# Decoder kernel, first self attention: projections as three products of rounded halves, weights split in the first batch and kept in memory

## The chip, the core and the metric

One core of a Trainium2 chip runs the whole program. The metric is the device time of one execution in microseconds; three runs of the kernel before gave 2879.1, 2882.16 and 2884.32, median 2882.16 us.

## What is computed

The model is a decoder of two layers over x of (4, 512, 512). The change touches only the first stage, the self attention of layer 0:

```python
q = x @ Wq + bq
k = x @ Wk + bk
v = x @ Wv + bv
q, k, v = (to_heads(q), to_heads(k), to_heads(v))
scores = jnp.einsum('bdsh,bdth->bdst', q, k) / SCALE
weights = jax.nn.softmax(scores, axis=-1)
feats = jnp.einsum('bdst,bdth->bdsh', weights, v)
feats = feats.transpose(0, 2, 1, 3).reshape(B, S, F)
return feats @ Wo + bo
```

Behind it come a cross attention, a mixture of experts, a second self and cross attention and a ternary feed-forward, all as before.

## The kernel before

`self_attention_0` runs the stage for one batch of 512 rows after the other (B = 4); the last batch is written out apart from the loop. All engines run their own program and meet in semaphores; the order of the work is that in which each engine's code is written.

**Projections.** For each batch there are twelve groups of products (g = 0 to 11): four of queries, four of keys (PARTS = 8 together), four of values. TensorE sums a group over four blocks of the contraction (L254, L257), in float32, into one of two banks, `mm[g % 2]`; it may start group g when the bank of g-2 has been read (`s.mm.free`). VectorE reads the bank with the bias added into `whole[:, g % 2]` (L401, L403). ScalarE rounds it to `high` (float32r, L340) and makes the copies that the scores need (L344): one half of `q_parts` per head, or both halves of `k_high`. VectorE subtracts `high` from `whole` (L391) into the low half of `q_parts`, or twice per head into `k_low`. This subtraction for group g-1 stands in VectorE's program in front of the reading of bank g. Value groups are added to `v_rows` directly (L407).

**Attention.** 32 tiles (`TILES`, 8 heads by 4) of scores, each as two products (L267, L268), maximum on VectorE (L411), exponential on ScalarE (L354), turned by TensorE (L109), weighted sums (L290), then the output projection (L316), which already uses three products of rounded halves (`feats_high`, `feats_low`, `wo_high`, `wo_low`) and is read on VectorE at L459. At the end of each but the last batch the next batch's x is turned and ScalarE copies it to `x_cols` (L332). VectorE ends a batch with the layernorm, for which GpSimd makes the root (L96).

**Transfers.** SP issues all loads of the stage at the start: x of batch 0, the three weights, all of x (4 MB, `x_tok`), `Wo`, biases. In each batch it then reloads `x_rows` (L226), loads two blocks of the second layer's output weights (L215) and stores their split halves (L220). GpSimd splits `Wo` in batch 0, then copies the experts' weights from memory to memory (L787 to L791) and at last issues the clearing of `moe_sorted` (L479), with batches 1 to 3's roots behind it.

Of the kernel before, what the change touches and what calls it, by code (L numbers as in the profile page):

```python
# [27 lines left out]
P = 128  # L28
# [105 lines left out]
def self_attention_0(nc, m, x, Wq, bq, Wk, bk, Wv, bv, Wo, bo, packed, a):  # L134
# [17 lines left out]
    PARTS = 2 * KD  # L152
    NEXT_X = TILES + 6
    Q0, SC = NT, TILES + 2 * NT
    TA, TV, MM = TILES // 2, TILES // 2, 3 * KD + 2 * GROUPS + NT
    with ExitStack() as ctx:
        sb, sem = allocator(nc, ctx, "a0")
        wq, wk, wv = (sb(n, [P, KD, D]) for n in ("wq", "wk", "wv"))
# [3 lines left out]
        x_rows, x_cols = sb("x_rows", [P, NT, D]), sb("x_cols", [P, KD, S])  # L162
# [6 lines left out]
        turned = [sb(f"turned_{i}", [P, NT, S]) for i in range(TURNED - 2)] + [x_rows, x_cols]  # L169
        turned = [x_rows] + [t for t in turned if t is not x_rows and t is not x_cols] + [x_cols]  # L170
        spare = turned[1:TURNED - 1]
        wo = spare[2]
        feats_high, feats_low = q_parts[:, 0:KD, :], q_parts[:, KD:2 * KD, :]
        feats = sb("feats", [P, NT, D])
        zeros = sb("zeros", [P, LATENT])
# [11 lines left out]
        s.whole_ready, s.high_ready, s.high_done, s.low_done = (sem(n) for n in ("whole_ready", "high_ready", "high_done", "low_done"))  # L187
        s.var_ready, s.rstd_ready = sem("var_ready"), sem("rstd_ready")
# [5 lines left out]
        block = ctx.enter_context(nc.Block())  # L194

        @block.sync
        def _(sp):
# [25 lines left out]
            with sp.Fori(0, B - 1) as b:  # L223
# [10 lines left out]
        def _(pe):  # L234
# [8 lines left out]
            def batch(b, last_one):  # L243
                F0 = NT + TILES if last_one else TILES + 2 * NT
                pe.wait_ge(s.sc.free, b * SC + s.sc.size + Q0)
                for g in range(3 * KD):
                    pe.wait_ge(s.mm.free, b * MM + g + 1)
                    c = g % KD
                    if c == 0:
                        pe.wait_ge((w_q, w_k, w_v)[g // KD], 32)  # L250
# [8 lines left out]
                    last.then_inc(s.mm.full, 1)  # L259
                pe.wait_ge(s.high_done, b * PARTS + PARTS)  # L260
# [67 lines left out]
        def _(act):  # L328
            def keep_x(use):
                for j in range(NT):  # L330
                    act.wait_ge(s.sc.full, use + j + 1)
                    act.copy(x_cols[:, :, j * P:(j + 1) * P], blocks_of(sc[j], KD)).then_inc(s.sc.free, 1)  # L332

            def batch(b, last_one):
# [42 lines left out]
            with act.Fori(0, B - 1) as b:  # L377
                batch(b, False)
# [3 lines left out]
        def _(dve):  # L382
            with dve.Fori(0, B) as b:
# [83 lines left out]

        @block.gpsimd
        def _(pool):
            pool.wait_ge(w_out, 32)  # L470
# [8 lines left out]
            pool.dma_start(packed.sorted.rearrange("(t p) d -> p t d", p=P), zeros[:].unsqueeze(1).to_broadcast([P, packed.sorted_tiles, LATENT])) \  # L479
# [284 lines left out]
class Packed:  # L764


    def __init__(self, nc, ctx):
# [5 lines left out]
        self.qkv1 = nc.dram_tensor("split_qkv", ((HEADS1 + 2 * KV_HEADS1), P, 2, KD, HD1), F32, kind="Internal").ap()  # L773
        self.wo1 = nc.dram_tensor("split_out", (HEADS1, P, 2, D), F32, kind="Internal").ap()
# [2193 lines left out]
```

## Time and profile before

| What | us |
|---|---|
| runs, median (lowest, highest) | 2882.16 (2879.1, 2884.32) |
| span of the profiled execution | 2871.8 |
| median above the span | 10.4 |
| TensorE busy | 2673.5 (93%) |
| VectorE busy | 1806.2 (63%) |
| ScalarE busy | 1420.3 (49%) |
| GpSimd busy | 294.5 (10%) |
| projections of batch 0, first product to first score | 12.05 to 54.79 |

The profile states the span of its execution, from the first instruction to the last; a whole execution's time has what lies around it as well, and the page gives no other time for it. "PE" is TensorE, "DVE" VectorE, "ACT" ScalarE, "POOL" GpSimd, "SP" the engine that issues most transfers; a "q" behind a name is that engine's sequencer. A span is printed for the products of a group together, with the count behind "x"; a float32 product of 512 columns stands there as two records. The granted clock is a share of 2.4 GHz.

### The profile page before, as it was taken

Reading aid. Unit: us, or ns where it says so; the run is one execution under the profiler, and the core shown is the slowest. Engines: PE = TensorE matmul, PEld = TensorE weight load, DVE = VectorE, ACT = ScalarE, POOL = GpSimd, SP = SyncE. Lnnn points to the kernel's source line nnn. Section 1 sums busy time; section 2 is a strip of 40 time slices with the busy share of each in tenths; the row PEclk is TensorE's granted clock in tenths of the full one; section 3 lists DMA queues with packets and bytes.
Section 4 is the critical chain, followed back from the end, with each engine's and each line's share of the span. In section 5 each row is a group of like instructions: output and inputs, shape, how many; then the busy total and the mean of one; then the engine's idle time right before and its main releaser. Section 6 shows DMA issues by size and latency. Waiting matters only on the chain. (4 is left out here: it accounts for less than half of the span.)

```text
span 2871.8 us, 40570 instructions
## 1 busy us (share of the span) xinstructions
PE 2673.5 (93%) x12750; PEld 1685.2 (59%) x12750; DVE 1806.2 (63%) x3475; ACT 1420.3 (49%) x2978; POOL 294.5 (10%) x399
## 2 busy tenths in 40 slices
PE   8999997979999987999999999997999999997898
PEld 4555554444588863677777777775545455443444
DVE  5666674654543326756755756754777777775676
ACT  4454463322133322554553653743577676664665
POOL 1230003001711114000000000001110101000000
PEclk9999998989999999999999999998899999999999
DMA  3395105541687754323223223211000000001000
GB/s 140 86 123 143 58 15 184 186 141 54 200 277 234 248 184 148 115 103 109 73 106 110 68 104 124 66 67 59 5 6 6 5 2 5 2 2 71 26 23 30
DMA packets 114169, 266.30 MB, mean 93 GB/s; under 512 B 14464, under 2 KB 37008, under 8 KB 113200
## 3 DMA queue, kind: packets, MB, share of 16 engines
q1 hardware_dynamic: 97152, 211.16, 22.2%
q0 software_dynamic: 16816, 52.64, 7.8%
q8 instruction: 104, 1.70, 0.2%
q14 instruction: 97, 0.79, 0.1%
HBM read 208.97 MB, written 58.48 MB: 93 GB/s over the span
## 5 line engine op out<-in xcount | busy, mean ns | idle before, releaser
L2506 DVE TENSOR_REDUCE x_neg_max<-bank 128x1 f32<-128x512 f32 x512 | 327.1, 684 | 99.7 <-PE bank L2351 99.2
L2458 ACT ACTIVATE x_weights<-bank 128x512 f32<-128x512 f32 x512 | 279.1, 599 | 127.8 <-PE bank L2362 122.9
L1885 ACT ACTIVATE a_probs<-bank,a_neg_max 128x128 f32<-128x128 f32 (+3 forms) x256 | 136.1, 532 | 206.0 <-DVE a_neg_max L1979 202.0
L1785 PE MATMUL bank<-a_x_high,a_weights 128*128 128x512 f32 x640 | 218.3, 404 | 8.2 <-DMA a_weights<-split_qkv 2.3
L109 PEld LDWEIGHTS bank<-all_ident,a_probs 128*128 128x128 f32 x1200 | 151.5, 140 | 85.0 <-issue 47.0
L109 PE MATMUL bank<-all_ident,a_probs 128*128 128x128 f32 x1200 | 193.3, 273 | 3.0 <-ACT a_probs_t L1877 2.2
L1877 ACT COPY a_probs_t<-bank 128x128 f32<-128x128 f32 (+3 forms) x256 | 107.6, 420 | 144.2 <-PE bank L109 143.8
L1820 PE MATMUL bank<-a_k_cols,a_q_cols 128*128 128x128 f32 (+3 forms) x512 | 176.7, 434 | 0.4 <-DVE a_q_cols L1928 0.2
L1849 PE MATMUL bank<-a_wo,a_att_high 128*128 128x512 f32 x512 | 162.1, 398 | 3.9 <-DVE a_q_cols L1928 2.9
L1510 DVE TENSOR_TENSOR moe_acc<-bank,moe_acc 128x512 f32 x79 | 54.6, 692 | 171.1 <-PE bank L1176 170.5
L1165 PE MATMUL bank<-moe_gh_cols,moe_item 128*128 128x256 f32 x632 | 151.8, 383 | 3.0 <-DMA moe_item<-moe_items 2.7
L1176 PE MATMUL bank<-moe_item,moe_wide 128*128 128x256 f32 x632 | 149.4, 379 | 0.0
L1832 PE MATMUL bank<-a_probs_t,a_v_rows 128*128 128x512 f32 (+3 forms) x512 | 148.6, 433 | 0.0
L1264 ACT ACTIVATE moe_wide<-bank,moe_item 128x256 f32<-128x256 f32 x158 | 66.3, 471 | 161.6 <-PE bank L1165 129.1
L1785 PEld LDWEIGHTS bank<-a_x_high,a_weights 128*128 128x128 f32 x640 | 121.3, 189 | 39.6 <-issue 6.2
L1891 ACT ACTIVATE a_probs<-a_probs,a_inv_sum 128x128 f32<-128x128 f32 (+3 forms) x256 | 142.0, 555 | 2.7 <-DVE a_inv_sum L1984 2.7
L2351 PE MATMUL bank<-x_k_cols,x_q_cols 64*128 64x512 f32 x512 | 136.6, 498 | 3.5 <-DVE x_neg_max L2506 3.4
L1979 DVE TENSOR_REDUCE a_neg_max<-bank 128x1 f32<-128x128 f32 (+3 forms) x256 | 125.7, 491 | 18.8
L2384 PE MATMUL bank<-x_weights,x_v_rows 128*17 128x512 f32 x1024 | 135.7, 603 | 0.0
L1165 PEld LDWEIGHTS bank<-moe_gh_cols,moe_item 128*128 128x128 f32 x632 | 118.1, 191 | 22.9 <-DMA moe_item<-moe_items 7.4
L2362 PE MATMUL bank<-x_q_cols,x_k_cols 64*128 64x512 f32 x512 | 128.1, 419 | 3.2 <-ACT x_weights L2458 2.8
L1176 PEld LDWEIGHTS bank<-moe_item,moe_wide 128*128 128x128 f32 x632 | 119.9, 190 | 16.8 <-issue 0.3
(413 smaller groups left out, 5437.0 us busy)
## 6 DMA issues: line engine op xcount, KB each, us to landing
a_weights<-split_qkv SPq DMA_DIRECT2D x80, 512.0 KB, 3.6
moe_item<-moe_items SPq DMA_DIRECT2D x79, 257.0 KB, 3.8
moe_item<-moe_items SPq DMA_DIRECT2D x79, 256.0 KB, 3.7
a_wo<-split_out SPq DMA_DIRECT2D x8, 2048.0 KB, 7.8
a_wo<-split_out SPq DMA_DIRECT2D x16, 1024.0 KB, 9.9
split_qkv<-x_qkv_parts SPq DMA_DIRECT2D x12, 1024.0 KB, 5.1
moe_items<-in_L_ffn_e_w POOLq DMA_DIRECT2D x40, 256.0 KB
split_out<-a_turned SPq DMA_DIRECT2D x8, 1024.0 KB, 4.0
```

What stands on the lines that cost most here:

```text
L109: last = pe.transpose(bank[:, c * P:(c + 1) * P], rows[:, c * P:(c + 1) * P], ident)
L1165: last = pe.matmul(bank(("hidden", i))[:, c * TOKENS:(c + 1) * TOKENS], weight[:, k, c * P:(c + 1) * P], x_now[:, i % 2, k * TOKENS:(k + 1 ...
L1176: last = pe.matmul(bank(("item", i))[:, j * LATENT:(j + 1) * LATENT], hid[:, i % 2, c * TOKENS + j * P:c * TOKENS + (j + 1) * P], weight[: ...
L1785: last = pe.matmul(mm[g % 2], weight[:, k, :], x[:, k, :], start=n == 0, stop=n == 3 * KD - 1)
L1820: pe.matmul(sc[n % 4][:, 0:t], q_cols[:, h % 2, j * P:t], k_cols[:, h // GROUP, 0:t], start=True, stop=True).then_inc(s.sc.full, 1)
L1832: last = pe.matmul(mm[g % 2][:, c * P:], v_rows[:, c, kv * HD1:(kv + 1) * HD1], probs_t[:, n % 2, c, c * P:], start=c == 0, stop=c == NT - 1)
L1849: last = pe.matmul(mm[g % 2], att[:, at, j * P:(j + 1) * P], wo[:, at, part, :], start=h == first and att is att_high and part == 0, stop= ...
L1885: act.activation(probs[:, n % SLOTS, 0:t], sc[n % 4][:, 0:t], ACT.Exp, bias=neg_max[:, n:n + 1], accum_out=row_sum[:, n:n + 1]).then_inc(s ...
L1891: act.activation(probs[:, i % SLOTS, 0:t1], probs[:, i % SLOTS, 0:t1], ACT.Copy, scale=inv_sum[:, i:i + 1]).then_inc(s.probs_ready, 1)
L2351: pe.matmul(score_banks[slot % 3], q_cols[rows, u % 2, pair, j * P:(j + 1) * P], k_cols[rows, u % 2, pair, :], start=True, stop=True).then ...
L2458: act.activation(weights[:, chunk % 2, k, :], weight_banks[slot % 2], ACT.Exp).then_inc(s.weight.free, 1)
L2506: dve.tensor_reduce(neg_max[:, g % 2, j, h:h + 1], score_banks[slot % 3], AX.X, ALU.max, negate=True) \
```

## The change

The three projections are computed as high·high + low·high + high·low: x is kept as `x_high` (ScalarE, float32r) and `x_low` (VectorE, the remainder), each weight as twelve pieces of two halves (pieces 0 to 3 of `Wq`, 4 to 7 of `Wk`, both by columns; 8 to 11 of `Wv`, by rows). A buffer of five slots, `pieces`, holds them: piece p lives in slot p % 5. In batch 0, which is now written out apart, ScalarE rounds each piece and VectorE subtracts; five pieces are made at the start and piece g+5 after group g. SP stores each made piece to `split_qkv0` in memory, and a slot is made anew only when its old piece is stored. For batches 1 to 3 SP loads the pieces from there: 0 to 4 after group 11 of the batch before, g+5 after group g. The raw `Wq` and `Wk` land in buffers used later for turned weights, `Wv` in `probs`. A value group needs all of pieces 8 to 11.

Besides: for keys ScalarE makes two of the four half copies, then signals `high_ready`, then makes the other two; the cast to `high` is gone there. VectorE writes `k_low` for only one half of the partitions, the other half is zeroed once. `x_low` is made on VectorE in step 41 of the 48 of the attention loop. The clearing of `moe_sorted` writes the same 6 MB in runs of 512 bytes instead of 1 KB.

```diff
-        wq, wk, wv = (sb(n, [P, KD, D]) for n in ("wq", "wk", "wv"))
+        pieces = sb("pieces", [P, PIECE_SLOTS, 2, D], F32R)
...
-        x_rows, x_cols = sb("x_rows", [P, NT, D]), sb("x_cols", [P, KD, S])
+        x_rows, x_high = sb("x_rows", [P, NT, D]), sb("x_high", [P, KD, S], F32R)
+        with ExitStack() as until_turned:
+            last_turned = until_turned.enter_context(nc.sbuf_tensor("a0_last_turned", [P, NT, S], F32))
+        x_low = sb("x_low", [P, KD, S], F32R)
...
+        wq, wk, wo = spare
+        wv = probs[:, 0:KD, :]
...
+            def load_piece(p):
+                sp.dma_start(pieces[:, p % PIECE_SLOTS].rearrange("p l n -> p (l n)").bitcast(F32), packed.qkv0[p].rearrange("p l n -> p (l n)")) \
+                  .then_inc(s.piece_in[p % PIECE_SLOTS], 16)
+
+            def next_pieces(b):
+                sp.wait_ge(s.mm.full, b * MM + PIECES)
+                for p in range(PIECE_SLOTS):
+                    load_piece(p)
+
+            def rest_of_pieces(b):
+                for p in range(PIECE_SLOTS, PIECES):
+                    sp.wait_ge(s.mm.full, b * MM + p - PIECE_SLOTS + 1)
+                    load_piece(p)
...
+            for p in range(PIECES):
+                sp.wait_ge(s.piece_in[p % PIECE_SLOTS], p // PIECE_SLOTS * 16 + 16)
+                sp.dma_start(packed.qkv0[p].rearrange("p l n -> p (l n)"), pieces[:, p % PIECE_SLOTS].rearrange("p l n -> p (l n)").bitcast(F32)) \
+                  .then_inc(s.piece_out[p % PIECE_SLOTS], 16)
+            for i in range(PIECE_SLOTS):
+                sp.wait_ge(s.piece_out[i], held(i) * 16)
+            next_pieces(0)
+            between(0)
+            with sp.Fori(1, B - 1) as b:
+                rest_of_pieces(b)
+                next_pieces(b)
+                between(b)
+            rest_of_pieces(B - 1)
...
+                def piece_ready(p):
+                    slot = p % PIECE_SLOTS
+                    pe.wait_ge(s.piece_in[slot], b * (held(slot) * 16) + p // PIECE_SLOTS * 16 + 16)
...
+                    if g < PARTS:
+                        piece_ready(g)
                     for k in range(KD):
-                        if g < PARTS:
-                            w = (wq, wk)[g // KD]
-                            last = pe.matmul(mm[g % 2], w[:, k, c * P:(c + 1) * P], x_cols[:, k, :],
-                                             start=k == 0, stop=k == KD - 1)
-                        else:
-                            last = pe.matmul(mm[g % 2], x_cols[:, k, c * P:(c + 1) * P], wv[:, k, :],
-                                             start=k == 0, stop=k == KD - 1)
+                        if g == PARTS:
+                            piece_ready(PARTS + k)
+                        for n, (w_part, x_part) in enumerate(((0, x_high), (0, x_low), (1, x_high))):
+                            start, stop = k == 0 and n == 0, k == KD - 1 and n == 2
+                            if g < PARTS:
+                                last = pe.matmul(mm[g % 2], piece_part(g, w_part)[:, k, :], x_part[:, k, :], start=start, stop=stop)
+                            else:
+                                last = pe.matmul(mm[g % 2], x_part[:, k, c * P:(c + 1) * P], piece_part(PARTS + k, w_part), start=start, stop=stop)
...
+            def high_piece(p):
+                if p in (0, KD, PARTS):
+                    act.wait_ge((w_q, w_k, w_v)[p // KD], 32)
+                if p >= PIECE_SLOTS:
+                    act.wait_ge(s.mm.full, p - PIECE_SLOTS + 1)
+                    act.wait_ge(s.piece_out[p % PIECE_SLOTS], p // PIECE_SLOTS * 16)
+                act.copy(piece_part(p, 0), raw_piece(p)).then_inc(s.piece_high, 1)
+
+            def batch(b, last_one, first_one=False):
                 F0 = NT + TILES if last_one else TILES + 2 * NT
                 for g in range(PARTS):
                     act.wait_ge(s.whole_ready, b * PARTS + g + 1)
-                    if g >= 2:
-                        act.wait_ge(s.low_done, b * PARTS + g - 1)
-                    act.copy(high[:, g % 2, :], whole[:, g % 2, :]).then_inc(s.high_ready, 1)
-                    for u in range(2):
-                        for half in range(2 if g >= KD else 1):
-                            to = k_high if g >= KD else q_parts
-                            last = act.copy(to[half * HD:(half + 1) * HD, 2 * (g % KD) + u, :], whole[u * HD:(u + 1) * HD, g % 2, :])
-                    last.then_inc(s.high_done, 1)
+                    if g < KD:
+                        if g >= 2:
+                            act.wait_ge(s.low_done, b * PARTS + g - 1)
+                        act.copy(high[:, g % 2, :], whole[:, g % 2, :]).then_inc(s.high_ready, 1)
+                        for u in range(2):
+                            last = act.copy(q_parts[0:HD, 2 * g + u, :], whole[u * HD:(u + 1) * HD, g % 2, :])
+                        last.then_inc(s.high_done, 1)
+                    else:
+                        for other in range(2):
+                            for u in range(2):
+                                half = (u + other) % 2
+                                last = act.copy(k_high[half * HD:(half + 1) * HD, 2 * (g % KD) + u, :], whole[u * HD:(u + 1) * HD, g % 2, :])
+                            last.then_inc((s.high_ready, s.high_done)[other], 1)
+                    if first_one and g + PIECE_SLOTS < PIECES:
+                        high_piece(g + PIECE_SLOTS)
...
+            def low_x(b):
+                for j in range(NT):
+                    tile = slice(j * P, (j + 1) * P)
+                    dve.wait_ge(s.x_high_ready, b * NT + j + 1)
+                    dve.tensor_tensor(x_low[:, :, tile], blocks_of(sc[j], KD), x_high[:, :, tile].bitcast(F32), ALU.subtract).then_inc(s.sc.free, 1)
+
+            def low_piece(p):
+                dve.wait_ge(s.piece_high, p + 1)
+                dve.tensor_tensor(piece_part(p, 1), raw_piece(p), piece_part(p, 0).bitcast(F32), ALU.subtract) \
+                   .then_inc(s.piece_in[p % PIECE_SLOTS], 16)
...
-                            for to in ([q_parts[HD:P, head, :]] if g <= KD else [k_low[0:HD, head, :], k_low[HD:P, head, :]]):
-                                last = dve.tensor_tensor(to, whole[rows, (g - 1) % 2, :], high[rows, (g - 1) % 2, :].bitcast(F32), ALU.subtract)
+                            to, part = (q_parts[HD:P, head, :], high[rows, (g - 1) % 2, :]) if g <= KD else (k_low[0:HD, head, :], k_high[rows, head, :])
+                            last = dve.tensor_tensor(to, whole[rows, (g - 1) % 2, :], part.bitcast(F32), ALU.subtract)
...
+                    if first_one and g + PIECE_SLOTS < PIECES:
+                        low_piece(g + PIECE_SLOTS)
                 for i in range(TILES + FEATS_LAG + 1):
+                    if i == NEXT_X + NT - 1 and not last_one:
+                        low_x(b + 1)
...
-            pool.dma_start(packed.sorted.rearrange("(t p) d -> p t d", p=P), zeros[:].unsqueeze(1).to_broadcast([P, packed.sorted_tiles, LATENT])) \
+            pool.dma_start(packed.sorted.rearrange("(p t) (u d) -> p (t u) d", p=P, u=2), zeros[:].unsqueeze(1).to_broadcast([P, 2 * packed.sorted_tiles, LATENT // 2])) \
```

ScalarE at the start of the stage and in the first query groups, before:

```order
L332 COPY a_x_cols<-bank 128x4x128 x4
L377 UNCONDITIONAL_BRANCH
L377 ISA
L340 CAST a_high<-a_whole 128x512
L344 CAST a_q_parts<-a_whole 64x512 x2
L337 REGISTER_ALU
L340 CAST a_high<-a_whole 128x512
L344 CAST a_q_parts<-a_whole 64x512 x2
L337 REGISTER_ALU
```

and now (`a_turned` there is the raw `Wq`, in one of the buffers of that name):

```order
L387 CAST a_x_high<-bank 128x4x128 x4
L395 CAST a_pieces<-a_turned 128x512 x5
L404 CAST a_high<-a_whole 128x512
L406 CAST a_q_parts<-a_whole 64x512 x2
L395 CAST a_pieces<-a_turned 128x512
L404 CAST a_high<-a_whole 128x512
L406 CAST a_q_parts<-a_whole 64x512 x2
L395 CAST a_pieces<-a_turned 128x512
L404 CAST a_high<-a_whole 128x512
```

The cast of a piece now stands behind each group's copies, in front of the cast to `high` of the next group.

SP from the last start loads on, before:

```order
L206 DMA all_x_tok<-in_x 128x16x512
L207 DMA a_turned<-in_L_attn_Wo 128x4x512
L208 DMA a_bo_row<-in_L_attn_bo 128x512
L223 UNCONDITIONAL_BRANCH
L225 ISA
L226 ISA
L226 DMA a_x_rows<-all_x_tok 128x2048
L212 ISA
L215 ISA
L215 DMA a_whole<-in_L_attn_Wo 128x2x512
L215 ISA
L215 DMA a_high<-in_L_attn_Wo 128x2x512
```

and now:

```order
L227 DMA all_x_tok<-in_x 128x16x512
L228 DMA a_turned<-in_L_attn_Wo 128x4x512
L229 DMA a_bo_row<-in_L_attn_bo 128x512
L267 DMA split_qkv<-a_pieces 128x1024 x12
L245 DMA a_pieces<-split_qkv 128x1024 x5
L261 DMA a_x_rows<-all_x_tok 128x2048
L236 DMA a_whole<-in_L_attn_Wo 128x2x512
L236 DMA a_high<-in_L_attn_Wo 128x2x512
L241 DMA split_out<-a_turned 128x2x1024 x2
L273 UNCONDITIONAL_BRANCH
```

Twelve stores of pieces stand behind the start loads, then the five loads for batch 1; in the loop seven more loads stand in front of these five.

## Rows read from the trace of the kernel before

**Rows 1.** the profile's page, part 1: busy us (share of the span) xinstructions

```profile
PE 2673.5 (93%) x12750; PEld 1685.2 (59%) x12750; DVE 1806.2 (63%) x3475; ACT 1420.3 (49%) x2978; POOL 294.5 (10%) x399
```

**Rows 2.** TensorE's timeline, batch 0: start us, us, engine, line, operation, count

```profile
12.05 13.97 PE L254 MATMUL bank<-a_x_cols,a_wq 128*128 128x512 f32 x32 [0.87 <-ACT a_x_cols L332]
...
54.79 0.79 PE L267 MATMUL bank<-a_k_high,a_q_parts 128*128 128x512 f32 x1
```

**Rows 3.** the same view, batch 1

```profile
123.79 13.89 PE L254 MATMUL bank<-a_x_cols,a_wq 128*128 128x512 f32 x32
137.52 13.90 PE L254 MATMUL bank<-a_x_cols,a_wk 128*128 128x512 f32 x32
...
166.95 0.79 PE L267 MATMUL bank<-a_k_high,a_q_parts 128*128 128x512 f32 x1
```

**Rows 4.** timeline, VectorE reading the output projection's banks, batch 0

```profile
115.59 0.69 DVE L459 TENSOR_TENSOR all_x_tok<-bank,all_x_tok 128x512 f32 x1 [0.16 <-PE bank L316]
...
118.40 0.68 DVE L459 TENSOR_TENSOR all_x_tok<-bank,all_x_tok 128x512 f32 x1
```

**Rows 5.** timeline, a key group (batch 0), then two query groups (batch 1)

```profile
34.00 0.75 DVE L403 TENSOR_SCALAR a_whole<-bank,a_bk_col 128x512 f32<-128x512 f32 x1 [0.24 <-issue]
...
35.36 2.50 ACT L344 CAST a_k_high<-a_whole 64x512 fp32r<-64x512 f32 x4
35.48 2.79 DVE L391 TENSOR_TENSOR a_k_low<-a_whole,a_high 64x512 fp32r<-64x512 f32 x4 [0.73 <-ACT a_high L340]
...
38.51 0.75 DVE L403 TENSOR_SCALAR a_whole<-bank,a_bk_col 128x512 f32<-128x512 f32 x1 [0.24 <-issue]
...
132.34 0.75 DVE L401 TENSOR_SCALAR a_whole<-bank,a_bq_col 128x512 f32<-128x512 f32 x1 [0.18 <-issue]
...
135.45 0.75 DVE L401 TENSOR_SCALAR a_whole<-bank,a_bq_col 128x512 f32<-128x512 f32 x1 [0.23 <-issue]
```

**Rows 6.** SP's issue, its landing, and 5 us windows (last: granted clock, DMA share, GB/s)

```profile
10.18 0.43 SPq L206 DMA_DIRECT2D all_x_tok<-in_x  x1
...
all_x_tok<-in_x SPq DMA_DIRECT2D x1, 4096.0 KB, 17.5
...
25.00:30.00 5.00, 5.00 (x13) 2.28 (x12) 3.12 (x5) 1.98 (x4) 0.00 (x0) 1.00 1.04 385
30.00:35.00 5.00, 5.00 (x13) 2.22 (x12) 3.74 (x6) 3.15 (x6) 0.00 (x0) 1.00 0.02 7
```

**Rows 7.** DMA issues from 300 to 310 us: KB each, us to landing

```profile
a_x_rows<-all_x_tok SPq DMA_DIRECT2D x1, 1024.0 KB, 5.2
```

**Rows 8.** timeline of GpSimd, and the landing of its last issue

```profile
127.03 0.95 POOL L787 DMA_DIRECT2D moe_items<-in_L_ffn_e_w  x1
...
238.67 2.28 POOL L479 DMA_DIRECT2D moe_sorted<-a_zeros  x1 [70.12 <-issue]
...
moe_sorted<-a_zeros POOLq DMA_DIRECT2D x1, 6144.0 KB, 22.7
```

**Rows 9.** SP's timeline; DMA issues and queues, 185 to 200, then 200 to 220 us

```profile
189.19 0.53 SPq L226 DMA_DIRECT2D a_x_rows<-all_x_tok  x1
...
q1 hardware_dynamic: 10, 0.08, 4.2%
a_x_rows<-all_x_tok SPq DMA_DIRECT2D x1, 1024.0 KB, 21.8
a_whole<-in_L_attn_Wo SPq DMA_DIRECT2D x1, 512.0 KB, 30.4
...
q1 hardware_dynamic: 580, 1.84, 58.1%
q0 software_dynamic: 619, 1.68, 51.9%
```

**Rows 10.** timeline of VectorE, end of batch 0's attention

```profile
107.89 0.69 DVE L427 COPY a_products<-bank 128x512 f32<-128x512 f32 x1 [4.11 <-PE bank L290]
```

**Rows 11.** window of 2 us, end of batch 1 (columns as in rows 6)

```profile
222.00:224.00 2.00, 1.64 (x8) 1.64 (x9) 1.43 (x3) 0.54 (x1) 0.00 (x0) 0.61 0.83 120
```

More of the change, by code:

```diff
@@ L152, in self_attention_0 @@
     PARTS = 2 * KD
+    PIECES, PIECE_SLOTS = 3 * KD, 5
     NEXT_X = TILES + 6
@@ L167, in self_attention_0 @@
         probs, products = sb("probs", [P, SLOTS, S]), sb("products", [P, S])
[L169 to L172, printed above, removed]
+        spare = [sb(f"turned_{i}", [P, NT, S]) for i in range(TURNED - 2)]
+        turned = [x_rows] + spare + [last_turned]
+        wq, wk, wo = spare
+        wv = probs[:, 0:KD, :]
         feats_high, feats_low = q_parts[:, 0:KD, :], q_parts[:, KD:2 * KD, :]
         feats = sb("feats", [P, NT, D])
-        zeros = sb("zeros", [P, LATENT])
+        zeros = sb("zeros", [P, LATENT // 2])
         out_rows = [whole[:], high[:].bitcast(F32)]
@@ L187, in self_attention_0 @@
         s.whole_ready, s.high_ready, s.high_done, s.low_done = (sem(n) for n in ("whole_ready", "high_ready", "high_done", "low_done"))
+        s.piece_in, s.piece_out = ([sem(f"{n}_{i}") for i in range(PIECE_SLOTS)] for n in ("piece_in", "piece_out"))
+        s.piece_high, s.x_high_ready, s.low_zeroed = sem("piece_high"), sem("x_high_ready"), sem("low_zeroed")
         s.var_ready, s.rstd_ready = sem("var_ready"), sem("rstd_ready")
@@ L194, in self_attention_0, with held, raw_piece, piece_part @@
         block = ctx.enter_context(nc.Block())
+        def held(slot):
+            return len(range(slot, PIECES, PIECE_SLOTS))
+        def raw_piece(p):
+            if p < PARTS:
+                return (wq, wk)[p // KD][:, :, p % KD * P:(p % KD + 1) * P]
+            return wv[:, p - PARTS, :]
+        def piece_part(p, part):
+            to = pieces[:, p % PIECE_SLOTS, part, :]
+            return to.rearrange("p (k n) -> p k n", k=KD) if p < PARTS else to
         @block.sync
@@ L221, in store_out, with between @@
                       .then_inc(s.out_stored, 16)
-            with sp.Fori(0, B - 1) as b:
+            def load_piece(p):
[9 more added lines that the diff above has]
+                    load_piece(p)
+            def between(b):
                 sp.wait_ge(x_tok_loaded, 16)
@@ L248, in batch @@
                     c = g % KD
[L249 to L250 removed]
+                    if g < PARTS:
+                        piece_ready(g)
                     for k in range(KD):
[L252 to L258 removed]
+                        if g == PARTS:
[6 more added lines that the diff above has]
+                                last = pe.matmul(mm[g % 2], x_part[:, k, c * P:(c + 1) * P], piece_part(PARTS + k, w_part), start=start, stop=stop)
                     last.then_inc(s.mm.full, 1)
+                pe.wait_ge(s.low_zeroed, 1)
                 pe.wait_ge(s.high_done, b * PARTS + PARTS)
@@ L331, in keep_x @@
                     act.wait_ge(s.sc.full, use + j + 1)
-                    act.copy(x_cols[:, :, j * P:(j + 1) * P], blocks_of(sc[j], KD)).then_inc(s.sc.free, 1)
-            def batch(b, last_one):
+                    act.copy(x_high[:, :, j * P:(j + 1) * P], blocks_of(sc[j], KD)).then_inc(s.x_high_ready, 1)
+            def high_piece(p):
[6 more added lines that the diff above has]
+            def batch(b, last_one, first_one=False):
                 F0 = NT + TILES if last_one else TILES + 2 * NT
@@ L376, in _ @@
             keep_x(0)
-            with act.Fori(0, B - 1) as b:
+            for p in range(PIECE_SLOTS):
+                high_piece(p)
+            batch(0, False, True)
+            with act.Fori(1, B - 1) as b:
                 batch(b, False)
@@ L382, in _, with batch @@
         def _(dve):
-            with dve.Fori(0, B) as b:
+            def low_x(b):
[7 more added lines that the diff above has]
+                   .then_inc(s.piece_in[p % PIECE_SLOTS], 16)
+            def batch(b, last_one, first_one=False):
                 for g in range(3 * KD):
@@ L466, in _ @@
                 layernorm(dve, st, b, m, s)
+            low_x(0)
+            for p in range(PIECE_SLOTS):
+                low_piece(p)
+            batch(0, False, True)
+            with dve.Fori(1, B - 1) as b:
+                batch(b, False)
+            batch(B - 1, True)
         @block.gpsimd
         def _(pool):
+            pool.memset(k_low[HD:P, :, :].bitcast(F32), 0.0).then_inc(s.low_zeroed, 1)
             pool.wait_ge(w_out, 32)
@@ L773, in __init__ @@
         self.qkv1 = nc.dram_tensor("split_qkv", ((HEADS1 + 2 * KV_HEADS1), P, 2, KD, HD1), F32, kind="Internal").ap()
+        self.qkv0 = nc.dram_tensor("split_qkv0", (3 * KD, P, 2, D), F32, kind="Internal").ap()
         self.wo1 = nc.dram_tensor("split_out", (HEADS1, P, 2, D), F32, kind="Internal").ap()
```

## The prediction

> **What bounds the kernel now.** The page's busy shares come first: TensorE is busy 93% of the span [rows 1], so the first question is whether the products of this change get shorter. The timeline of TensorE shows the projections of batch 0 from 12.05 us to the first scores at 54.79 [rows 2], those of batch 1 from 123.79 to 166.95; there four groups of query products (16 products, recorded as 32) take until 137.52, 3.43 us a group [rows 3]. What a group of three rounded products costs stands in the output projection, which is already written so: its banks are read at 115.59 and 118.40, 2.80 us for twelve products [rows 4]. So TensorE alone would gain 3.43 - 2.80 = 0.63 us a group, 7.6 a batch, 30 us in all.
>
> The next view says who really paces the groups. VectorE and ScalarE hand one buffer back and forth: VectorE makes `whole` (0.75), ScalarE rounds it (VectorE idles 0.73 for that; its half copies take 2.50 for four, 0.62 each), VectorE subtracts (2.79 for the four of a key group, 0.69 each; a query group has two) and only then takes the next bank. From `whole` to `whole` this is 3.11 us for queries and 4.51 for keys [rows 5]. In batch 1 VectorE starts late besides, behind the layernorm. So after batch 0 it is this chain that sets the pace, not TensorE, until the last value groups. I stepped groups, banks and this chain through with these durations: it gives 54.9 and 167.1 us for the two first scores, against 54.79 and 166.95 read. I use the same stepping below.
>
> **Batches 1 to 3, if every piece is there in time.** Query groups: the chain stays at 3.11, gain 0. Key groups: two low subtractions instead of four (-1.39), but `high_ready` now comes after two half copies instead of one cast (+0.62), so 4.51 - 0.77 = 3.74; four of them give 3.1. The last two value groups run on TensorE alone: 2 x 0.63 = 1.3. Together -4.2 us a batch (stepping: 162.7 instead of 166.95).
>
> **Batch 0.** Three things are added in front of or inside the chain.
> 1. Start. ScalarE casts piece 0 after its four copies, VectorE makes four `x_low` and low piece 0: first product at 13.2 instead of 12.05.
> 2. One more piece per group. For g = 0 to 6 ScalarE's cast of piece g+5 (0.62) and VectorE's subtraction (0.69) stand between `whole` and the next low part, and the cast stands behind all ScalarE copies of the group. A query step is 0.75 + 0.08 + 3 x 0.62 + 0.62 + 0.03 + 0.69 + 1.39 + 0.24 = 5.66, a key step 6.29. Stepping with this alone: first scores at 67.9, +13.0.
> 3. The wait for the store. Piece 5 goes into slot 0, so ScalarE must wait until piece 0 has been stored. SP puts this store behind all start loads in the same queue: the 4 MB load of x is issued at 10.18 and lands 17.5 us later, and the DMA engines run at 385 GB/s until 30 us and are idle behind that [rows 6]. 0.5 MB more at that rate is 1.4 us: I take 32 us for the first store. ScalarE is ready for it at about 19. While it stands there, the rounding of group 1 is queued behind it, VectorE waits in low piece 5, and TensorE stops when both banks are full, at 21.7. `whole` 1 ends at 35.8, `whole` 4 at 52.8, `whole` 7 at 71.7, the value groups end at 81.0.
>
> So the first scores of batch 0 move from 54.9 to 81.0: **+26.1**. Later stores have 5 us each and hold nothing up.
>
> **Batch 1: the pieces against GpSimd's copies.** SP loads pieces 5 to 11 (0.5 MB each) while the groups run, each after the group that frees its slot. In an empty queue that is harmless: 1 MB lands in 5.2 us [rows 7], and there are five groups (15 us) to spare for most, some 7 us for piece 11. But GpSimd starts its copies of the expert weights at 127.03, just as batch 1 begins, and their traffic holds its queue until 238.67 [rows 8]. What an SP load costs beside them: x_rows, issued at 189.19, lands after 21.8 us, the next 0.5 MB after 30.4; from 185 to 200 the SP queue moved 10 packets, from 200 to 220 1.84 MB, which is 92 GB/s [rows 9]. I take 9.5 us until a load begins, then 5.7 us a piece. Pieces 5 and 6 are issued before the copies have filled the queue. Piece 7, issued at 132.7, lands at 147.9, 8 at 153.6, 11 at 170.7. Value group 0 needs all of 8 to 11, so it ends at 171.4, and the scores start at 179.8 instead of 166.95: **+12.9**. The bounds: -4.2 if nothing is delayed, +27 at 8.5 us a piece (what the 0.5 MB behind took).
>
> Without the 9.5 us in front, still at 5.7 us a piece, piece 11 lands at 161.8, the scores start at 171.0 and the term is +4.0; that is for the rivals. The rows speak against it: 10 packets in 15 us, then 580 in 20 us beside 619 of the other queue [rows 9], so a load does wait before it gets its share.
>
> The Trainium skill, DMA: Bandwidth & Descriptors (Queues, rings and completion order), says that each engine takes turns between the queues at every packet. By that rule a piece would begin at once, which is the +4.0. The rows agree with turns after 200 us and not before.
>
> **The tail of batch 1.** Behind these come the five pieces of the next batch (28 us), x_rows and the two halves of the output weights on the same slow queue. x_rows then lands around 229, wanted at 228; the output weights around 241 to 248, wanted at 242. +4, bounds 0 and +10.
>
> **Batch 2.** The clearing of `moe_sorted` (6 MB, 22.7 us) is issued just at its start, at 238.67 [rows 8], and its source runs are halved to 0.5 KB. It is a memory write with nothing to wait for but the engines; a wait of 4.5 us in front of a piece costs under 1 us, one of 9.5 us gives +20. I take -3. **Batch 3** has no neighbour: -4.3.
>
> **Small terms.** `low_x` puts four subtractions into VectorE's gap of 4.11 us in front of the copy of `products` at 107.89 [rows 10]; the last of them must wait for ScalarE's last x copy and can push this copy by at most its own 0.69. I take half of it, three times: +1. GpSimd's clearing of half of `k_low` and its doubled run count are hidden before the first scores and behind batch 1. Clock: between 222 and 224 us, behind TensorE's gaps at the end of batch 1, the granted clock was 0.61 of full, so part of it at 1.2 GHz [rows 11]. Batch 0 leaves TensorE half idle; there the chain covers even groups at half clock (2 x 2.80 = 5.6 against 5.66), only the last value groups show it: +2, bounds 0 and 6.
>
> **Sum**: 26.1 + 12.9 + 4 - 3 - 4.3 + 1 + 2 = +38.7 us. The profile gives a span of 2871.8 us, 10.4 below the median of the runs; start and end are not touched, so the profiled execution stands for the median and I add to that: 2882.2 + 38.7 = **2920.9**.
>
> **Rivals.**
> - *TensorE paces after all* (faster). If the hand-over between VectorE and ScalarE did not bind, because `whole` and `high` have two buffers each, every group would give 0.63: 2882 - 30 = 2852. It decides once the chain is under 2.80 us a step. Against it: steps of 3.11 and 4.51 while both banks were full [rows 5]. Something faster than before by a few us also needs the store wait to vanish. 0.04.
> - *All transfers hidden.* The store of piece 0 overtakes, the pieces come in time: 13.0 - 12.7 + 1 = +1.3, 2883.5. For it: 0.5 MB alone is short. Against: the queue was never idle before 30 us, and the 4 MB load in front of the stores took its full 17.5 us [rows 6]. 0.07.
> - *Only the first store waits.* Batch 1's pieces get their share at once (+4.0) or are not delayed (-4.2), no tail: 26.1 + 4.0 - 3 - 4.3 + 3 = +26 down to +17: 2899 to 2908. 0.17.
> - *The contention is worse.* 8.5 us a piece in batch 1, +10 in the tail, or +20 in batch 2: 2940 to 2965. GpSimd's next layernorm step stands behind the clearing, which is issued only when the copies have drained; if more SP traffic stretches these, batch 2 starts late too. 0.17.
> - *Forecast* as above, 2908 to 2940: 0.55.
>
> **How the numbers follow.** About 0.2%, 6 us, is what a measurement of this kernel can tell from no change. Faster comes from the first rival alone, 0.04. No change: the second, 0.06, its rest being slower by a little. Slower: 0.90. The range must hold 8 in 10: it leaves out the first two rivals and the end of the fourth, and goes from 2892 to 2950.
>
> **What would show it.** In the new profile: the first scores of batch 0 near 81 us, with ScalarE idle from 19 to 32 in front of the cast of `pieces`, released by a DMA; group steps of 5.7 and 6.3 us behind that. Groups of 2.80 us on TensorE with gaps between them. In batch 1 a wait of 15 to 20 us in front of the first value group, released by a DMA into `pieces`; landings of 15 us and more there and under 5 in batch 3. Batch 3's projections 4.3 us shorter than before. The forecast is wrong if the first stores land before 25 us, if the pieces of batch 1 land in under 8 us, or if the stages behind the first attention change their length.

## The result, and the profile after

| | median us | lowest to highest | runs |
|---|---|---|---|
| before | 2883.24 | 2879.1 to 2892.22 | 4 |
| changed | 2917.08 | 2915.11 to 2921.52 | 4 |

The ratio is 1.0122, 95% interval 1.0101 to 1.0143: slower by 1.2%. The forecast was 2920.9 us in a range of 2892 to 2950, slower with 0.90. It held, but against the profiled execution of the kernel before two of its terms were too small and something else made up for them, as the stages show.

The span of the changed kernel's profiled execution is 2913.6 us. Its page, part 1, answers [rows 1]:

```profile
PE 2659.1 (91%) x12942; PEld 1728.9 (59%) x12942; DVE 1802.9 (62%) x3471; ACT 1419.1 (49%) x2974; POOL 299.6 (10%) x400
```

Windows by stage: first self attention, all up to the second cross attention, this, the rest. The kernel before (us, busy time and count of each engine, granted clock, DMA share, GB/s):

```profile
0.00:469.70 469.70, 434.55 (x1809) 246.64 (x1809) 310.87 (x492) 226.61 (x492) 58.90 (x81) 0.99 0.41 92
469.70:2005.40 1535.70, 1421.70 (x6147) 1024.42 (x6146) 868.06 (x1876) 637.40 (x1556) 167.08 (x255) 0.97 0.42 137
2005.40:2662.70 657.30, 626.06 (x3653) 318.72 (x3654) 476.27 (x862) 431.51 (x783) 59.84 (x49) 0.97 0.04 13
2662.70:2871.80 209.10, 191.24 (x1144) 95.43 (x1142) 150.97 (x246) 124.80 (x149) 8.69 (x16) 0.98 0.06 21
```

and the changed kernel:

```profile
0.00:519.20 519.20, 428.32 (x2001) 293.88 (x2001) 306.07 (x488) 226.07 (x489) 63.73 (x82) 0.92 0.51 131
519.20:2054.50 1535.30, 1420.53 (x6146) 1023.49 (x6146) 868.97 (x1876) 636.89 (x1555) 166.64 (x254) 0.97 0.42 137
2054.50:2705.80 651.30, 620.34 (x3653) 316.73 (x3654) 476.92 (x861) 431.31 (x783) 60.60 (x50) 0.98 0.04 13
2705.80:2913.60 207.80, 189.91 (x1145) 94.75 (x1142) 150.94 (x246) 124.79 (x149) 8.66 (x16) 0.99 0.06 21
```

The first stage takes 49.5 us more, not 38.7, with TensorE busy 6.2 us less: all of it is waiting. The stages behind give back 7.7, 6.0 of them in the second cross attention, whose program is the same. Each of these figures sets one execution against one other. A second profiled execution of the kernel before, shown further down, has its first stage end at 480.7 instead of 469.7, and its later stages are 14.7 us shorter in sum.

Marks in TensorE's timeline, first product of the projections, first score and first turning of `feats`, give each part of a batch (us; "out" is from there to the next batch's first product):

| | projections, batches 0 to 3 | attention, 0 to 3 | out, 0 to 2 |
|---|---|---|---|
| before | 42.7, 43.2, 44.8, 43.0 | 55.6, 55.4, 55.4, 53.1 | 13.4, 14.7, 13.4 |
| changed | 68.1, 64.1, 39.6, 38.6 | 55.1, 66.1, 55.1, 52.6 | 14.6, 13.4, 14.6 |

**Batch 0.** ScalarE, VectorE and TensorE in the changed kernel's timeline, against [rows 2, 5]:

```profile
32.61 0.62 ACT L395 CAST a_pieces<-a_turned 128x512 fp32r<-128x512 f32 x1 [11.89 <-DMA split_qkv<-a_pieces]
...
35.55 0.75 DVE L485 TENSOR_SCALAR a_whole<-bank,a_bq_col 128x512 f32<-128x512 f32 x1
...
41.17 0.75 DVE L485 TENSOR_SCALAR a_whole<-bank,a_bq_col 128x512 f32<-128x512 f32 x1 [0.17 <-issue]
...
52.45 0.75 DVE L487 TENSOR_SCALAR a_whole<-bank,a_bk_col 128x512 f32<-128x512 f32 x1 [0.20 <-PE bank L310]
...
58.70 0.75 DVE L487 TENSOR_SCALAR a_whole<-bank,a_bk_col 128x512 f32<-128x512 f32 x1 [0.17 <-issue]
```

```profile
36.35 0.80 PE L310 MATMUL bank<-a_x_high,a_pieces 128*128 128x512 f32 x1 [12.85 <-DVE a_whole L485]
```

The cast of piece 5 waits 11.89 us for the store of piece 0; VectorE and TensorE stand behind it. Then the steps are 5.62 (queries) and 6.25 (keys).

**Batch 1.** TensorE's timeline, then the landings of two pieces issued between 170 and 185 us and of `x_rows`, issued behind 225:

```profile
182.93 0.79 PE L310 MATMUL bank<-a_x_high,a_pieces 128*128 128x512 f32 x1 [10.15 <-DMA a_pieces<-split_qkv]
...
192.37 0.79 PE L312 MATMUL bank<-a_pieces,a_x_high 128*128 128x512 f32 x1 [3.22 <-DMA a_pieces<-split_qkv]
...
203.94 0.79 PE L312 MATMUL bank<-a_pieces,a_x_high 128*128 128x512 f32 x1 [5.33 <-DMA a_pieces<-split_qkv]
...
215.06 0.40 PE L322 MATMUL bank<-a_k_high,a_q_parts 128*128 128x512 f32 x1
...
270.23 1.11 PE L109 MATMUL bank<-all_ident,a_x_rows 128*128 128x128 f32 x4 [7.95 <-DMA a_x_rows<-all_x_tok]
```

```profile
a_pieces<-split_qkv SPq DMA_DIRECT2D x2, 512.0 KB, 29.1
...
a_x_rows<-all_x_tok SPq DMA_DIRECT2D x1, 1024.0 KB, 33.3
```

The queues (packets, MB, share of 16 engines; q1 carries SP's loads, q0 GpSimd's copies) from 162 to 166, 166 to 170, 175 to 180, and 195 to 200 us:

```profile
q0 software_dynamic: 174, 0.52, 99.1%
q1 hardware_dynamic: 29, 0.09, 11.1%
...
q0 software_dynamic: 114, 0.32, 82.0%
q1 hardware_dynamic: 17, 0.07, 27.2%
...
q1 hardware_dynamic: 156, 0.57, 72.3%
q0 software_dynamic: 147, 0.41, 31.6%
...
q0 software_dynamic: 207, 0.57, 82.1%
q1 hardware_dynamic: 63, 0.21, 22.8%
```

From 162 to 170 SP's queue moves 46 packets beside 288 of the copies, although up to four pieces are under way; then it gets half the packets and some 110 GB/s. Near its end it falls to 63 packets in 5 us and then, while TensorE still waits for the last piece (until 203.94), nearly stops: from 200 to 205 us the two queues have

```profile
q0 software_dynamic: 176, 0.50, 114.9%
q1 hardware_dynamic: 2, 0.00, 0.2%
```

The Trainium skill, DMA: Bandwidth & Descriptors (Queues, rings and completion order), has the engines take turns between queues at each packet; this trace agrees from 175 to 180 us and disagrees from 162 to 170, 46 against 288.

The windows give TensorE's clock in these gaps (last three columns: granted clock, DMA share, GB/s). It falls to a mean of 0.56 of full, so for most of that window it is at 1.2 GHz, with TensorE busy 3.29 us of 10:

```profile
180.00:190.00 10.00, 6.17 (x15) 4.28 (x15) 0.75 (x1) 0.95 (x2) 10.00 (x16) 0.61 1.01 192
190.00:200.00 10.00, 3.29 (x6) 1.66 (x6) 1.37 (x2) 1.51 (x3) 5.58 (x9) 0.56 1.05 163
```

**Batch 3**, without a neighbour. VectorE's timeline and the landing of pieces 5 to 11:

```profile
424.95 0.75 DVE L487 TENSOR_SCALAR a_whole<-bank,a_bk_col 128x512 f32<-128x512 f32 x1 [0.17 <-issue]
...
428.61 0.75 DVE L487 TENSOR_SCALAR a_whole<-bank,a_bk_col 128x512 f32<-128x512 f32 x1 [0.17 <-issue]
```

```profile
a_pieces<-split_qkv SPq DMA_DIRECT2D x7, 512.0 KB, 3.6
```

A key step is 3.66 us, VectorE waiting for no bank: the hand-over sets it.

### The profile page after: what moved, and what is told of

Its sections match the earlier page's. It is cut to its first block and busy times, and to the rows that moved or that the text cites. A ratio compares the mean times of both kernels' runs of the same rounds, so it can differ in the third digit from the quotient of the medians.

```text
span 2913.6 us, 40788 instructions
## 1 busy us (share of the span) xinstructions
PE 2659.1 (91%) x12942; PEld 1728.9 (59%) x12942; DVE 1802.9 (62%) x3471; ACT 1419.1 (49%) x2974; POOL 299.6 (10%) x400
```

## The experiments

Theory: the loss is the store wait and one more piece per group in batch 0, and GpSimd's copies beside the loads in batch 1; what is left is set by the hand-over of `whole`, not by TensorE. Each "next stage" below is the profile's start of the first cross attention: 469.7 us before, 519.2 changed. Each ratio is against the kernel before on the same chip. Chips differ: on that of the first three runs and of the moved subtraction the kernel before has a median of 2899.92 us, so whole times are compared by their ratios and stages by their traces.

### Stores of the pieces ahead of the start loads

```diff
-            sp.dma_start(m.x_tok[:], ...)
-            sp.dma_start(wo[:], chunked(Wo))
-            sp.dma_start(bo_row[:], ...)
...
             for p in range(PIECES):
                 ... store of piece p
+            sp.dma_start(m.x_tok[:], ...)
+            sp.dma_start(wo[:], chunked(Wo))
+            sp.dma_start(bo_row[:], ...)
```

> The changed kernel, but SP issues the 4 MB load of x, Wo and its bias behind the twelve stores of pieces instead of in front of them. Theory (ScalarE waits 11.9 us in batch 0 only because the first store stands behind the start loads): the gap in front of the cast of piece 5 closes, first scores of batch 0 at 68 us instead of 81.3, the rest unchanged, total 13 us less, about 2904. Rival (a store to memory is slow by itself, or later stores hold ScalarE up as well): the gap stays or moves to pieces 6 to 9, total within 4 us of 2917.

Measured 2924.58 us, ratio 1.0099 (1.0065 to 1.0133). First score of batch 0 at 70.8 instead of 81.3, next stage at 501.5. ScalarE's timeline has the cast of piece 5 without a wait:

```profile
20.46 0.62 ACT L395 CAST a_pieces<-a_turned 128x512 fp32r<-128x512 f32 x1
```

12.15 us earlier than before the edit; 1.6 of them go again in the value groups, where the granted clock is 0.72. So the queue order costs 10.5 us in batch 0. The next stage comes 17.7 us sooner and not 13, mostly because batch 1 now meets the copies at another moment (projections 61.1 for 64.1, attention 63.8 for 66.1), where the rest was expected unchanged. The ratio alone does not show the gain: its interval includes the changed kernel's 1.0122.

### GpSimd's copies spread over batches 0 to 2, the clearing in batch 3

```diff
-            layernorm_rstd(pool, st, 0, m, s)
-            pack_experts(pool, packed, a)
-            ... clearing
-            with pool.Fori(1, B) as b:
+            for b in range(B):
+                if b > 0:
+                    pool.wait_ge(s.mm.full, b * MM + 3 * KD)
+                if b < B - 1:
+                    pack_experts(pool, packed, a, b, B - 1)
+                else:
+                    ... clearing
                 layernorm_rstd(pool, st, b, m, s)
```

The copies now start only when a batch's projections have ended, a third of them each time. First in the changed kernel:

> The changed kernel, but GpSimd's copies of the expert weights are issued in three parts, each behind the projections of batch 0, 1 and 2, and the clearing of moe_sorted behind those of batch 3. Theory (the loads of pieces are slow only beside these copies): projections of batch 1 take 39 us instead of 64.1, its attention and output part 70 to 71 instead of 79.5, batch 2's projections stay near 39; total 32 to 36 us less, about 2883. Rival (loads of 0.5 MB from memory at this pace are too slow for the groups whatever runs beside them): batch 1 keeps most of its 21 us, landings stay above 10 us, total less by under 10.

Measured 2905.13 us, ratio 1.0015 (0.9998 to 1.0032). Projections of batch 1 are 39.2 us instead of 64.1, its attention 55.1 instead of 66.1, next stage 484.3, 34.9 us sooner. By the two ratios (1.0122 and 1.0015) the whole kernel gains some 31 us, a little under the 32 to 36 expected. Twelve pieces issued from 135 to 200 us land in

```profile
a_pieces<-split_qkv SPq DMA_DIRECT2D x12, 512.0 KB, 3.7
```

Then the same in the kernel before, as a control:

> Control: the kernel before with the same spreading of GpSimd's copies. Theory: it has no loads in the projections that the copies could delay, so the time stays within 4 us of 2883. Rival (the copies slow the stage by another way, such as the engines' access to memory or GpSimd's late root): 10 us or more less, and then e2's gain is not the pieces' alone.

Measured 2890.88 us, ratio 0.998 (0.9964 to 0.9996), next stage 468.0: 1.7 us. Its batch 1 is as it was: projections 43.1 us, attention 55.4. The 24.9 and 11.0 us that batch 1 of the changed kernel gets back are thus the meeting of the copies with the loads that the change adds. The whole kernel is 9.0 us faster than before on this chip, more than the 4 expected, so the spreading has a worth of its own. A part of it is the layernorm's root on GpSimd, which in the kernel before comes directly behind the clearing in batch 2, at 241.00 us, and here waits for VectorE (first line before, second this run):

```profile
241.00 1.04 POOL L96 TENSOR_TENSOR a_ln_rstd<-a_ln_var_eps,all_minus_half 128x4 f32<-128x4 f32 x1
...
239.21 1.04 POOL L96 TENSOR_TENSOR a_ln_rstd<-a_ln_var_eps,all_minus_half 128x4 f32<-128x4 f32 x1 [57.12 <-DVE a_ln_var_eps L86]
```

These 1.8 us are the 1.7 of the stage; runs further down have the root later still.

### Two products instead of three

```diff
+                            if g < PARTS and n == 1:
+                                continue
```

> The changed kernel without the product of the rounding remainder of x with the high halves of the weights (x_low by w_high) in the query and key groups: it leaves that part of the computation out, so two products of 128x512 in place of three in each of these passes; loads, conversions, buffers and everything else stay. Theory (the projections of a batch are set by the chain of loads, two conversions on ScalarE and the subtraction on VectorE, not by TensorE): the projections of batch 3 stay at 38.6 us within 0.5, those of batches 0 and 1 at 68 and 64 within 3, the first score of batch 0 comes at 81, and the next stage starts at 519 within 5, as in the changed kernel. Rival (TensorE paces the groups): 32 products of 0.233 us fewer in a batch, 7.5 us, so the projections of batch 3 come to about 31 us and the next stage starts some 30 us sooner.

This kernel leaves `x_low` by `w_high` out for queries and keys, so it is no candidate, only a measure of who paces. Measured 2909.01 us (one run), beside 2878.09 before on that chip. Projections of batch 3 are 38.6 us, not a tenth less for 32 products less; batch 0 69.1. The rival that TensorE paces falls. Missed: the next stage starts at 509.5, not 519, since batch 1 took 60.5 and 59.5 us for 64.1 and 66.1; how the copies and the loads meet varies with where they fall.

### The subtraction behind the next bias addition

```diff
                 for g in range(3 * KD):
-                    if 1 <= g <= PARTS:
-                        ... low part of group g-1
                     ... read bank g into whole or v_rows
+                    if 1 <= g <= PARTS:
+                        ... low part of group g-1
-                    if first_one and g + PIECE_SLOTS < PIECES:
-                        low_piece(g + PIECE_SLOTS)
+                    if first_one and 1 <= g <= PIECES - PIECE_SLOTS:
+                        low_piece(g + PIECE_SLOTS - 1)
```

> The changed kernel, but VectorE reads bank g before it makes the low part of group g-1 (and in batch 0 low piece g+4 instead of g+5), so that ScalarE's rounding runs beside VectorE instead of between two of its steps. Theory (the hand-over sets the pace): projections of batch 3 take 34.6 us instead of 38.6 (whole 0 at 6 us, then ten groups of 2.80), batch 2 the same, batch 1 stays bound by its loads, batch 0 saves 14 to 17 us behind its store wait; total 22 to 26 us less, about 2893. Rival (TensorE or the loads set the pace already): batch 3 stays at 38 to 39, total within 5 us of 2917.

Measured 2913.0 us, ratio 1.0041 (1.0022 to 1.0059), next stage 494.9. Projections 51.0, 60.4, 43.4 and 34.0: where the loads are in time, TensorE's twelve products of 2.80 us now pace, 4.6 us a batch less than 38.6. Batch 2 was expected at 34.6 as well and missed it: its pieces land in 11.4 us (median of eight) beside the clearing, and the first value group waits four times for one, 1.94 us at most. The groups now ask for them sooner; behind the waits the granted clock is 0.74.

### All three edits in the changed kernel

> The changed kernel with all three edits: stores in front of the late start loads, copies spread behind the projections, VectorE reading the next bank first. Theory (store wait, contention and hand-over are the whole loss, and without them TensorE paces the halves): projections of batch 0 take 44 to 48 us, of batches 1 to 3 34 to 35; the first stage ends about 22 us earlier than in the kernel before (469.7), and the total is 18 to 30 us less than before on the same chip (ratio 0.990 to 0.994). Rival (the pieces' loads or the splitting keep a price of their own): batches 1 to 3 at 38 or more, ratio 0.997 or above.

Measured 2837.55 us, ratio 0.9869 (0.9844 to 0.9894): faster than both kernels, and by more than expected (37.6 us less than before on that chip, for 18 to 30). Projections 39.1, 34.1, 34.1, 34.0, next stage 435.6; batch 0 had been put at 44 to 48. VectorE's timeline in batch 1 has bank after bank in 2.75 us, VectorE waiting for TensorE:

```profile
130.22 0.75 DVE L478 TENSOR_SCALAR a_whole<-bank,a_bq_col 128x512 f32<-128x512 f32 x1 [0.56 <-PE bank L310]
...
132.97 0.75 DVE L478 TENSOR_SCALAR a_whole<-bank,a_bq_col 128x512 f32<-128x512 f32 x1 [0.40 <-PE bank L310]
```

### The change's handling of keys alone, in the kernel before

The reordered half copies and the single subtraction of the diff above, with float32 products; then also the subtraction moved as in the edit above.

> The kernel before with one part of the change alone: ScalarE's two half copies then high_ready for keys, k_low for one half, the other zeroed; the projections stay in float32. Theory: key steps 3.74 instead of 4.51 us until TensorE's 3.43 a group binds; projections of batches 1 and 3 take 41.1 instead of 43.2 us, the total is 6 to 8 us less than before (ratio 0.9972 to 0.998). Rival (TensorE paces the float32 groups already): projections stay at 43, ratio 1.000.

> The kernel before with the keys' part and with VectorE reading the next bank first, float32 projections. Theory (behind the chain TensorE's 3.43 us a group is the floor): the same as e7 within 2 us, projections 41.2 us, since there is nothing left to gain from the chain. Rival (the hand-over still binds in e7): 3 us a batch less than e7.

Measured 2866.83 us, ratio 0.9968 (0.9953 to 0.9983), and 2867.11, ratio 0.9969 (0.9952 to 0.9987). Both have 40.8 us in batches 1 and 3. The simpler keys are worth 2.2 to 2.4 us a batch, and moving the subtraction nothing, because TensorE's 3.43 us a group then sets the pace. This also says what the halves alone gave in the changed kernel: with the same keys and the subtraction in its old place it has 38.6 us in batch 3, 2.2 less than 40.8. Batch 2 takes 49.2 and 51.4 us in these two, with VectorE waiting 8.53 and 9.20 us for the root.

### The kernel before, once more

> The kernel before, unchanged, for a profile on the same chip as the others of this call. Theory (differences behind the first stage are the chip's, not the kernel's): its first stage ends at 469 to 470 us as in the profile before, and its later stages take the same times as those of e7 and e8 within 5 us together. Rival (the kernel before is slower in later stages than all its variants): 8 us or more longer there.

Measured 2869.82 us with a span of 2868.1: a whole execution is 1.7 us above its span, as in the changed kernel (2915.34 and 2913.6). Its second cross attention takes 650.8 us; the 657.3 shown above was that execution's. The expectation for the first stage, 469 to 470, missed by 11 us:

```profile
480.74 0.63 PE L109 MATMUL bank<-all_ident,x_w_rows 128*128 128x128 f32 x4 [0.23 <-ACT x_x_cols L620]
```

The same kernel takes 44.6 us for batch 0's projections here (42.7 in the first profile), 17.8 for batch 1's output part (14.7), 49.7 for batch 2's projections (44.8) and 14.6 for its output part (13.4). Whether the chip or the single execution makes these 11.0 us is not shown. For the largest part, batch 2, GpSimd's and VectorE's timelines show why:

```profile
247.16 2.28 POOL L479 DMA_DIRECT2D moe_sorted<-a_zeros  x1 [76.75 <-issue]
249.45 1.06 POOL L96 TENSOR_TENSOR a_ln_rstd<-a_ln_var_eps,all_minus_half 128x4 f32<-128x4 f32 x1
```

```profile
250.55 1.91 DVE L89 TENSOR_SCALAR all_x_tok<-all_x_tok,a_ln_mean_var,a_ln_rstd  x4 [6.37 <-POOL a_ln_rstd L96]
```

The root for the layernorm stands behind the clearing, which is issued only when the copies have drained: at 247.16 us here, at 238.67 in the first profile. In the changed kernel it is issued at 288.06, before VectorE needs the root.

### What the halves are worth by themselves

The kernel before with the keys, the moved subtraction and the spread copies, and e6's kernel again on the same chip:

> The kernel before with all that the changed one got in e6_all_three except the projections as halves: the reordered key copies, the subtraction after the next bias addition, and the expert copies spread over three batches (its weights need no loads, so there are no stores to reorder). It asks whether the three products of halves pay in themselves once what stood round them is gone. Theory (TensorE's float32 products set the projections here, 40.8 us a batch, against 34.1 with halves): projections 40.8 in batches 1 to 3, about 42.5 in batch 0, the next stage starts near 463, and the total lies 20 to 28 us above that of e6's kernel on the same chip (6.7 us a batch less, as far as the clock lets it). Rival (the other edits made the gain of e6, the halves none): the total lies within 5 us of that of e6's kernel.

> The kernel of e6_all_three again, beside e10_before_unlocked_spread on one chip. Theory: projections 39, 34, 34 and 34 us, next stage at 436, total 0.985 to 0.989 of the kernel before. Rival (the gain was that chip's): 0.995 or more.

Measured 2854.62 us, ratio 0.9914 (0.9885 to 0.9944), and 2830.72, ratio 0.9832 (0.9812 to 0.9851): 23.9 us apart. The gain of all three edits is thus not one chip's. Projections are 40.8 against 34.1 us, the next stage starts at 457.4 (463 was expected) and 435.6. TensorE paces both, as VectorE's timeline of the first shows, 3.43 us from bank to bank:

```profile
132.19 0.75 DVE L401 TENSOR_SCALAR a_whole<-bank,a_bq_col 128x512 f32<-128x512 f32 x1 [1.08 <-PE bank L255]
...
135.62 0.75 DVE L401 TENSOR_SCALAR a_whole<-bank,a_bq_col 128x512 f32<-128x512 f32 x1 [1.09 <-PE bank L255]
```

## Why the prediction was right, and where it was not

- **Who paces the groups.** Right: not TensorE. Two products instead of three left 38.6 us as they were, and moving the subtraction out of the way made them 34.0. Key step 3.74 forecast, 3.66 and 3.72 read; batch 3 -4.3 forecast, -4.5 read. The split of this gain was off: 3.1 for the keys and 1.3 for the halves were forecast, and the run with the keys alone makes it 2.2 and 2.2, because float32 products bind at 3.43 us a group once the keys are simpler.
- **Batch 0, +26.1.** Right: the first score moved by 26.5. The store landed at about 32 us as forecast, the steps were 5.62 and 6.25 for 5.66 and 6.29. Stores first took 10.5 us of it away, close to the 13.1 that the two sums (81.0 and 67.9) put on this wait; the value groups at part clock are most of the difference.
- **Batch 1's projections, +12.9.** This term failed in size: +20.9. The mechanism was the one named, a load that first waits and then has some 5.5 us a piece (0.16 MB from 162 to 170 us, then 0.57 MB in five). But SP's queue nearly stopped a second time near its end (2 packets from 200 to 205 us), so the last piece came 52.9 us after the batch's first product (203.94 - 151.01) where 46.9 was forecast, and what lay behind took 11.1 us instead of 9.1, beginning at half clock. These are the missing 8. The sign said a wait of 15 to 20 us in front of the first value group; the longest, 10.15, stood in front of the last key group, and 11.5 in three waits inside the first value group.
- **The tail of batch 1, +4.** Too small as well: attention and output took 79.5 us for 70.1, +9.4, of which 7.95 is TensorE's wait for `x_rows`. It lands after 33.3 us; 21.8 was its time before [rows 9].
- **Batch 2, -3.** -5.2 read. The clearing did no harm. 1.7 of this has nothing to do with the groups: the root on GpSimd is late in the first profile of the kernel before (44.8 us for batch 2, 43.1 with the copies spread) and not in the changed kernel.
- **Small terms and clock, +3.** What is left of the 49.5 is +2.4: some 1.2 us more in each other output part, where TensorE's granted clock is lower (0.89 in that of batch 0, 1.00 before), and 0.3 to 0.6 less in each other attention.
- **The base.** The step "the profiled execution stands for the median" failed. An execution is 1.7 us above its span, so that one took some 2873.5 us, 9.7 below the median, where the changed kernel's was 1.7 below. Of the 49.5 us more in the first stage, 7.7 come back in stages that are the same in both and 8.0 in this: 33.8 between the medians. The forecast came within 4 us of the time because terms that were 10.8 too small met these 15.7 us, which have nothing to do with the change. That closeness is luck. Nor are the 10.8 themselves firm: against the second profiled execution of the kernel before, the changed kernel's first stage is 38.5 us longer (519.2 and 480.7), with batch 0's first score +24.6, batch 1's projections +20.9 and what lies behind them +6.3, batch 2 -10.1, batch 3 -4.5. The term of batch 1's projections was too small by either; how far the others were off, one execution of each kernel cannot say. By the prediction's own list the forecast was wrong if the stages behind changed their length; they did, by 7.7, but two executions of the kernel before differ there by 14.7, so this sign could not tell anything.
- **The rivals.** *TensorE paces* fell with the two-product run. *Only the first store waits* fell with the spread copies: 24.9 us in batch 1's projections and 11.0 in its attention. *Worse contention* named the right direction, but 2940 was not reached.

Open: why SP's queue is held off for some eight microseconds and then gets its share. The runs show that it goes with GpSimd's copies, not what in the engines does it.

## What to carry to other kernels

An edit that makes TensorE's products cheaper pays in full only when TensorE waits for nobody: read the step from buffer to buffer on the engines behind it first, since here the cheaper products alone gave 2.2 us a batch, and one subtraction moved by one place another 4.6. A buffer that is refilled from memory in each pass turns every unrelated transfer of that time into a possible wait: list what other queues run there, and move that traffic, or the refills, before judging the products. And a sum against a profiled execution should be set against that execution's own time; the median may lie elsewhere, and a stage of the same kernel may: here it ended at 469.7 and at 480.7 us.

## What was not expected of the hardware

- A 0.5 MB load that lands in 3.6 us alone took 29.1 us beside memory-to-memory copies, and the DMA engines moved only 163 to 192 GB/s in all then, at a busy share of 1.01 to 1.05, where the start loads had 385 [rows 6]. The busy share told nothing of the rate.
- A wait for pieces costs twice: the granted clock fell to 0.56 in the gaps, and behind the first gap the products stand 0.43 us apart (183.52 to 183.95), at 1.2 GHz, where 0.23 is usual.
